# Row minima subtracted by GpSimd and the exponential taken on the way out of PSUM, in a relative-position attention loop

## Chip, cores and metric
The kernel runs as one program on one core of a Trainium2 chip. Its time is that of the device in microseconds (us); lower is better. A core has TensorE (PE, its weight loads are listed as PEld), VectorE (DVE), ScalarE (ACT), GpSimd (POOL) and SyncE (SP), which run their own instruction queues and meet at semaphores, and 16 DMA engines.

## What is computed
The reference is one transformer block over x of 32 batches x 512 tokens x 256 channels: a layer norm, relative-position attention with 16 heads of 16 channels, and an expert layer (8 experts, each takes its 128 best tokens of the 512 of a batch, two products with GELU between, scatter-add). The attention is what matters here:

```python
content_score = jnp.einsum('bhsp,bhtp->bhst', q + u, k)
pos_score = jnp.einsum('bhsp,htp->bhst', q + v, pos)
pos_score = _relative_shift(pos_score)     # pad a column, reshape, drop a row
score = (content_score + pos_score) / jnp.sqrt(jnp.float32(P))
weights = jax.nn.softmax(score, axis=-1)
out = jnp.einsum('bhst,bhtp->bhsp', weights, val)
```

For each of 32 x 16 = 512 (batch, head) pairs the scores are a 512x512 float32 matrix.

## The kernel before
There are two phases, `attention_phase` and `ffn_phase`, with a barrier between them. The attention phase first normalises all batches (to some 185 us) and then runs `ITERS` = 16 unrolled bodies of `BH` = 32 heads (two batches). A head is worked on as TT = 4 tiles of 128 queries x 512 keys. Every engine has its own order, written out by hand in `body(i)`; `kk` is the head within the body and `n = i*BH + kk` its number.

One head passes these stages:

- `position` (PE, L988): four products of the queries with the positions into `xp`, half of the PSUM tensor `quad`, two tiles at a time, LEAD = 5 heads ahead. `x_evacuate` (ACT, L609) copies two tiles at once into a ring in SBUF; SP writes them to DRAM (`write_x`, L411) with rows of 513, and reads them back with rows of 512 (`read_x`, L421) into `shifted`, a ring of NX = 8 heads. This write and read is the relative shift. The read-back of a head follows BEHIND = 2 heads after its write in SP's order.
- `content` (PE, L999): four products of queries and keys into `sp_`, the other half of `quad`, with two banks; tile t waits until the add of tile t-2 is done. `add` (DVE, L761) forms (content + position) x -0.25 in place in `shifted` and the row minimum of it in `mn`.
- `exponential` (ACT, L614): per tile, exp(mn - x) in place in `shifted`.
- `turn` (PE, L1024 and L1025), LAG = 2 heads later: the tiles are transposed by TensorE in two halves of two key blocks; each half fills `tp`, a PSUM tensor of 128x1024 that exists once. `t_evacuate` copies it into `pt` in SBUF: half 0 by DVE (L770, 128x1024), half 1 by DVE (L772, 128x512) and ACT (L623, 128x512) together.
- `times_values` (PE, L1042), three heads behind: products with the values and a column of ones, into `op`; `o_evacuate` (ACT, L630) and `store_o` (SP) once in four heads. The division by the sum happens in the second phase.

Beside this, once in two to sixteen heads, run the projections of the next queries, keys and values (PE L933, L950), their spreading over the partitions (PE L917, L918, evacuated by DVE L734 and L741), and on GpSimd the splits of operands into a high and a low part: `keys` (L504, L506), `queries` (L495, L497) and `split_xt` (L514, L516). After the last body GpSimd issues eight indirect gathers (`gather_tokens`, L92) of the first tokens for the experts.

Of the kernel before, what the change touches and what calls it, by code (L numbers as in the profile page):

```python
# [7 lines left out]
ALU = mybir.AluOpType  # L8
ACT = mybir.ActivationFunctionType
# [11 lines left out]
TT = S // P  # L21
# [118 lines left out]
def attention_phase(nc, x, gate_w, w, w1, w2, consts, xn_d, xt_d, xs_d, att_d, sums_d, shared):  # L140
# [9 lines left out]
    LAG = 2  # L150
# [10 lines left out]
    with ExitStack() as ctx:  # L161
# [65 lines left out]
        def first_keys(n):  # L227

            at = n % 2 * TT
            return pt[:, at:at + 2].rearrange("p c (t r n) -> p (c t) r n", t=TT, r=2)  # L230

        def last_keys(r):
            by_rows = pt[:, 2:4].rearrange("p c (t r n) -> p (c t) r n", t=TT, r=2)
            return by_rows[:, :, r]
# [75 lines left out]
        exp_done = m.sem("exp_done")  # L310
        t_full = m.sem("t_full")
        t_out_dve = m.sem("t_out_dve")
        t_out_act = m.sem("t_out_act")
# [41 lines left out]
        with nc.Block() as block:  # L355
# [121 lines left out]
            def _(pool):  # L477
# [39 lines left out]

                split_xt(0, 0)
# [7 lines left out]
                def body(i):  # L526
                    last = isinstance(i, int) and i == ITERS - 1
                    for kk in range(BH):
                        t = kk // MH + 1
                        if kk % MH == 4 and not (last and t >= TILES):  # L530
                            keys(i, t)
# [17 lines left out]
            def _(act):  # L549
# [61 lines left out]
                def exponential(i, kk, t):  # L611

                    act.wait_ge(added, (i * BH + kk) * TT + t + 1)
                    act.activation(shifted[:, kk % NX, t], shifted[:, kk % NX, t], ACT.Exp, bias=mn[:, kk % NX, t:t + 1],  # L614
                                   scale=-1.0).then_inc(exp_done, 1)

                def t_evacuate(i, kk):

                    n = i * BH + kk
                    act.wait_ge(t_full, (n + 1) * TT)  # L620

                    wait(act, o_full, n)
                    act.activation(last_keys(1), tp[:, 1], ACT.Copy).then_inc(t_out_act, 1)  # L623
# [20 lines left out]
                exponential(0, 0, 0)  # L644

                def body(i):
                    first = isinstance(i, int) and i == 0
                    last = isinstance(i, int) and i == ITERS - 1
                    for kk in range(BH):
# [3 lines left out]
                        if not (first and kk == 0):  # L653
                            exponential(i, kk - 1, 1)
                            exponential(i, kk - 1, 2)
# [6 lines left out]
                        if not (first and kk == 0):  # L662
                            exponential(i, kk - 1, 3)
                            exponential(i, kk, 0)
                        if positions:
                            x_evacuate(i, kk + LEAD, 1)
                        if not (first and kk < LAG):
                            t_evacuate(i, kk - LAG)
# [5 lines left out]
                for t in range(1, TT):  # L674
                    exponential(ITERS, -1, t)
                for k in range(LAG):
                    t_evacuate(ITERS, k - LAG)
# [3 lines left out]
            def _(dve):  # L681
# [83 lines left out]
                def t_evacuate(i, kk, t):  # L765
                    n = i * BH + kk
                    dve.wait_ge(t_full, n * TT + (2, 4)[t])
                    wait(dve, o_full, n - 1 + t)
                    if t == 0:
                        dve.tensor_copy(first_keys(n), tp[:, :, :].rearrange("p r (k n) -> p k r n", k=2 * TT)).then_inc(t_out_dve, 1)  # L770
                    else:
                        dve.tensor_copy(last_keys(0), tp[:, 0]).then_inc(t_out_dve, 1)  # L772

# [74 lines left out]
                def body(i):  # L848
                    first = isinstance(i, int) and i == 0
                    last = isinstance(i, int) and i == ITERS - 1  # L850
                    for kk in range(BH):
                        even, odd = even_group(kk, last), odd_group(kk, last)
                        values = values_at(kk, last)
                        turning = not (first and kk < LAG)
                        add(i, kk, 1)
                        add(i, kk, 2)
                        if turning:
                            t_evacuate(i, kk - LAG, 0)
# [7 lines left out]
                        if turning:  # L866
                            t_evacuate(i, kk - LAG, 1)
# [12 lines left out]
                for k in range(LAG):  # L880
                    for t in range(2):
                        t_evacuate(ITERS, k - LAG, t)

            @block.tensor
            def _(pe):
# [125 lines left out]
                def turn(i, kk, half):  # L1011
                    n = i * BH + kk
                    pe.wait_ge(exp_done, (n + 1) * TT)

                    if half == 0:
# [610 lines left out]
```

## Time and profile before
| | |
|---|---|
| median of 3 runs | 4721.12 us (4718.89 to 4722.01) |
| profiled execution | 4728.36 us |
| its span on the core | 4726.5 us |
| busy in the span | PE 4382.3 us (93%), DVE 3530.2 (75%), ACT 3360.7 (71%), POOL 1261.8 (27%) |
| mean DMA rate | 294 GB/s over the span |

The profile shows one execution. A busy PE is not a PE at its peak, since matmuls are pipelined and their ends are modelled; spans on POOL are rough. The granted clock of TensorE is given as a share of 2.4 GHz, so that a stretch at 1.2 GHz reads 0.50. "Idle before" is the time in which an engine stood still just ahead of a group of instructions, with what ended it. The DMA share is the mean busy share of the 16 DMA engines; it can read a little over 1.

### The profile page before, as it was taken

The page shows a single profiled execution, that of the slowest core. Times are in us where ns is not written, and L with a number is a line of the kernel's source. Part 1 is how long each engine was busy: PE and PEld are TensorE (multiplying, and loading weights), DVE is VectorE, ACT ScalarE, POOL GpSimd, SP SyncE. Part 2 cuts the span into 40 slices and gives each one's busy share as a digit, 9 for nine tenths or more (in the row PEclk, how much of TensorE's full clock was granted, in tenths as well). Part 3 has the DMA queues.
Part 4 walks back from the last instruction along what each step waited for, and adds up shares of the span by engine and source line. Part 5 has one row for each costly group of instructions (what it writes and reads, how often), then busy time and mean ns, then how long its engine had stood idle before and what let it go on. Part 6 is the DMA issues. An engine that isn't in the chain of part 4 may idle for free. (4 is left out here: it accounts for less than half of the span.)

```text
span 4726.5 us, 126083 instructions
## 1 busy us (share of the span) xinstructions
PE 4382.3 (93%) x50100; PEld 3473.8 (73%) x50100; DVE 3530.2 (75%) x7282; ACT 3360.7 (71%) x5120; POOL 1261.8 (27%) x905
## 2 busy tenths in 40 slices
PE   7899999999989989989999999899999999999997
PEld 3466666666666667666667666589999999999997
DVE  7699999998999989999998989744454555434344
ACT  3599999998989999999898999744343433344454
POOL 0111111111111111111111111135565565644443
PEclk9799999999999999999999999999999999999999
DMA  8999999999999999999999999873454545433259
GB/s 330 343 387 387 391 386 385 397 385 383 390 390 388 386 387 390 392 386 385 388 395 382 394 388 385 320 247 77 117 144 110 140 117 128 108 55 86 45 169 311
DMA packets 467858, 1391.46 MB, mean 294 GB/s; under 512 B 59216, under 2 KB 136656, under 8 KB 467024
## 3 DMA queue, kind: packets, MB, share of 16 engines
q1 hardware_dynamic: 418128, 1316.25, 73.9%
q0 software_dynamic: 49152, 67.14, 8.0%
q8 instruction: 407, 6.67, 0.6%
q14 instruction: 171, 1.40, 0.1%
HBM read 708.93 MB, written 674.23 MB: 293 GB/s over the span
## 5 line engine op out<-in xcount | busy, mean ns | idle before, releaser
L761 DVE CUSTOM_DVE_ANT_0 att_shifted<-att_quad,att_shifted 128x512 f32<-128x512 f32 x2048 | 1336.6, 684 | 109.2 <-DMA att_shifted<-xs_d 70.3
L614 ACT ACTIVATE att_shifted<-att_shifted,att_mn 128x512 f32<-128x512 f32 x2048 | 1376.1, 733 | 0.6 <-DVE att_mn L761 0.6
L609 ACT ACTIVATE ring<-att_quad 128x1024 f32<-128x1024 f32 x1024 | 1055.5, 1031 | 261.4 <-PE att_quad L988 240.1
L999 PE MATMUL att_quad<-att_kd,att_qd 64*128 64x512 f32 x2048 | 848.5, 460 | 177.1 <-DVE att_mn L761 171.2
L1483 DVE TENSOR_TENSOR ffn_hp<-ring,ffn_hp 128x512 fp32r<-128x512 f32 x512 | 477.6, 933 | 685.3 <-ACT ring L1420 642.0
L1418 ACT ACTIVATE ffn_hp<-ffn_up 128x512 fp32r<-128x512 f32 x512 | 305.9, 597 | 914.5 <-PE ffn_up L1564 896.8
L988 PE MATMUL att_quad<-att_pos,att_qd 64*128 64x512 f32 x2048 | 862.5, 449 | 15.2 <-ACT ring L609 13.9
L1024 PEld LDWEIGHTS att_tp<-ident,att_shifted 64*128 64x128 f32 x8192 | 647.0, 142 | 272.3 <-ACT att_shifted L614 117.4
L1525 PE MATMUL ffn_yp<-ffn_w2p,ffn_hp 128*128 128x256 f32 x6144 | 827.8, 284 | 3.4 <-DVE ffn_hp L1483 1.7
L1525 PEld LDWEIGHTS ffn_yp<-ffn_w2p,ffn_hp 128*128 128x128 f32 x6144 | 798.7, 191 | 41.0 <-DVE ffn_hp L1483 3.8
L1564 PE MATMUL ffn_up<-ffn_xp,ffn_w1p 128*128 128x512 f32 x3072 | 795.1, 394 | 2.8 <-DVE ffn_xp L1443 2.8
L1024 PE MATMUL att_tp<-ident,att_shifted 64*128 64x64 f32 x8192 | 725.4, 229 | 68.4 <-DVE att_pt L770 23.8
L1025 PE MATMUL att_tp<-ident,att_shifted 64*128 64x64 f32 x8192 | 777.3, 232 | 2.4 <-issue 2.3
L1025 PEld LDWEIGHTS att_tp<-ident,att_shifted 64*128 64x128 f32 x8192 | 653.1, 142 | 18.5 <-issue 6.2
L770 DVE COPY att_pt<-att_tp 128x1024 f32<-128x1024 f32 x512 | 624.5, 1220 | 5.3 <-PE att_tp L1025 2.3
L999 PEld LDWEIGHTS att_quad<-att_kd,att_qd 64*128 64x128 f32 x2048 | 363.0, 190 | 354.1 <-DVE att_mn L761 259.4
L1358 POOL DMA_INDIRECT ffn_d<-ring,picks x256 | 431.8, 1687 | 696.2 <-DVE ring L1451 682.6
L1564 PEld LDWEIGHTS ffn_up<-ffn_xp,ffn_w1p 128*128 128x128 f32 x3072 | 546.4, 190 | 93.6 <-DVE ffn_xp L1443 3.2
L1042 PE MATMUL att_op<-att_pt,att_val 128*17 128x128 f32 x16384 | 601.6, 290 | 4.2 <-issue 3.8
L1042 PEld LDWEIGHTS att_op<-att_pt,att_val 128*17 128x17 f32 x16384 | 427.7, 102 | 60.0 <-issue 8.2
L504 POOL CAST att_kc<-att_qn 128x512 fp32r<-128x512 f32 x64 | 39.4, 616 | 1589.2 <-PE att_mp L918 1580.2
L988 PEld LDWEIGHTS att_quad<-att_pos,att_qd 64*128 64x128 f32 x2048 | 370.6, 190 | 92.2 <-issue 45.4
(125 smaller groups left out, 4992.6 us busy)
## 6 DMA issues: line engine op xcount, KB each, us to landing
xs_d<-ring SPq DMA_DIRECT2D x1024, 513.0 KB, 8.5
att_shifted<-xs_d SPq DMA_DIRECT2D x1024, 512.0 KB, 8.8
att_shifted<-in_L_attn_x_dram SPq DMA_DIRECT2D x32, 512.0 KB, 7.0
xn_d<-att_shifted SPq DMA_DIRECT2D x32, 512.0 KB, 6.4
xt_d<-att_shifted SPq DMA_DIRECT2D x32, 512.0 KB, 7.5
gathered<-xt_d SPq DMA_DIRECT2D x32, 512.0 KB, 9.7
att_d<-att_osb SPq DMA_DIRECT2D x512, 32.0 KB
ring<-in_L_ffn_w_dram SPq DMA_DIRECT2D x16, 1024.0 KB
```

The lines of the kernel that those rows point to most:

```text
L609: act.activation(xo[:, kk % NW, 2 * half:2 * half + 2, 1:S + 1], xp[:, :, :], ACT.Copy).then_inc(x_out, 1)
L614: act.activation(shifted[:, kk % NX, t], shifted[:, kk % NX, t], ACT.Exp, bias=mn[:, kk % NX, t:t + 1], scale=-1.0).then_inc(exp_done, 1)
L761: dve.tensor_tensor_reduce(out=shifted[:, kk % NX, t], in0=sp_[:, t % 2], in1=shifted[:, kk % NX, t], scale=-0.25, scalar=-NEG, op0=ALU.ad ...
L770: dve.tensor_copy(first_keys(n), tp[:, :, :].rearrange("p r (k n) -> p k r n", k=2 * TT)).then_inc(t_out_dve, 1)
L988: ins = pe.matmul(xp[:, t % 2, :], qd[rows, n // GH % ND, t * P:(t + 1) * P], pos[rows, kk // GH % NG8, :], start=True, stop=True)
L999: pe.matmul(sp_[:, t % 2, :], qd[rows, n // GH % ND, t * P:(t + 1) * P], kd[rows, kk // GH % 2, :], start=True, stop=True).then_inc(s_full, 1)
L1024: low = pe.transpose(tp[:, 0, at], shifted[0:ROWS, kk % NX, t, keys], ident[0:ROWS, 0:ROWS])
L1025: high = pe.transpose(tp[:, 1, at], shifted[ROWS:P, kk % NX, t, keys], ident[ROWS:P, ROWS:P])
L1042: ins = pe.matmul(op[32 * t:32 * t + HD + 1, kk % QH * P:(kk % QH + 1) * P], val[:, kk // H % 2, c, kk % H, :], pt[:, of_keys(n, c), t * P ...
L1483: dve.tensor_tensor(hp[:, g % 2, 1, f], hf[:, f % 2], hp[:, g % 2, 0, f].bitcast(F32), ALU.subtract).then_inc(h_low, 1)
L1525: ins = pe.matmul(yp[:, k % 2, 0:D], hp[:, g % 2, hi, f, k * CAP:(k + 1) * CAP], w2p[:, wi, f, :], start=(f == 0 and s == 0), stop=(f == F ...
L1564: ins = pe.matmul(up[:, f % 4, :], w1p[:, wi, c, f * P:(f + 1) * P], xp[:, g % 2, xi, c, :], start=(s == 0 and c == 0), stop=(s == 2 and c ...
```

## The change
The exponential no longer runs in place in SBUF. GpSimd subtracts the row minimum of each tile in place (`subtract_least`, four per head, first in its order for every head). TensorE transposes the differences. ACT then takes exp(-x) while it copies `tp` to `pt`: two instructions of 128x1024 per head, one per half, both from PSUM to SBUF. The four exponentials from SBUF to SBUF, DVE's two copies and ACT's copy are gone. The semaphores `exp_done`, `t_out_dve` and `t_out_act` give way to `lowered` and `t_out`. In `pt` both of a half's key blocks now have the same layout.

```diff
--- before.py
+++ after.py
@@ -224,14 +224,10 @@
         xp, sp_ = quad[:, 0], quad[:, 1]
         tp = m.ps("tp", [P, 2, S])
 
-        def first_keys(n):
-
-            at = n % 2 * TT
+        def turned_keys(n, half):
+
+            at = 2 if half else n % 2 * TT
             return pt[:, at:at + 2].rearrange("p c (t r n) -> p (c t) r n", t=TT, r=2)
-
-        def last_keys(r):
-            by_rows = pt[:, 2:4].rearrange("p c (t r n) -> p (c t) r n", t=TT, r=2)
-            return by_rows[:, :, r]
 
         def of_keys(n, c):
 
@@ -307,10 +303,9 @@
         x_shifted = [m.sem(f"x_shifted{k}") for k in range(NX)]
         s_full = m.sem("s_full")
         added = m.sem("added")
-        exp_done = m.sem("exp_done")
+        lowered = m.sem("lowered")
         t_full = m.sem("t_full")
-        t_out_dve = m.sem("t_out_dve")
-        t_out_act = m.sem("t_out_act")
+        t_out = m.sem("t_out")
         o_full = m.sem("o_full")
         o_out = m.sem("o_out")
         o_stored = [m.sem(f"o_stored{k}") for k in range(2)]
@@ -515,6 +510,12 @@
                     wait_alone(pool, xt_high, b + 1)
                     pool.tensor_tensor(xt[:, s, 1], xf[:, :, :], xt[:, s, 0].bitcast(F32), ALU.subtract).then_inc(xt_low, 1)
 
+                def subtract_least(i, kk, t):
+
+                    pool.wait_ge(added, (i * BH + kk) * TT + t + 1)
+                    pool.tensor_scalar(shifted[:, kk % NX, t], shifted[:, kk % NX, t], mn[:, kk % NX, t:t + 1], None,
+                                       ALU.subtract).then_inc(lowered, 1)
+
                 split_xt(0, 0)
                 queries(0, 0)
                 keys(0, 0)
@@ -527,6 +528,8 @@
                     last = isinstance(i, int) and i == ITERS - 1
                     for kk in range(BH):
                         t = kk // MH + 1
+                        for r in range(TT):
+                            subtract_least(i, kk, r)
                         if kk % MH == 4 and not (last and t >= TILES):
                             keys(i, t)
                         if kk % MH == 6 and t % 2 and not last:
@@ -608,19 +611,14 @@
                     act.wait_ge(x_full, (i * BH + kk) * 2 + half + 1)
                     act.activation(xo[:, kk % NW, 2 * half:2 * half + 2, 1:S + 1], xp[:, :, :], ACT.Copy).then_inc(x_out, 1)
 
-                def exponential(i, kk, t):
-
-                    act.wait_ge(added, (i * BH + kk) * TT + t + 1)
-                    act.activation(shifted[:, kk % NX, t], shifted[:, kk % NX, t], ACT.Exp, bias=mn[:, kk % NX, t:t + 1],
-                                   scale=-1.0).then_inc(exp_done, 1)
-
-                def t_evacuate(i, kk):
+                def exponential(i, kk, half):
 
                     n = i * BH + kk
-                    act.wait_ge(t_full, (n + 1) * TT)
-
-                    wait(act, o_full, n)
-                    act.activation(last_keys(1), tp[:, 1], ACT.Copy).then_inc(t_out_act, 1)
+                    act.wait_ge(t_full, n * TT + 2 * (half + 1))
+
+                    wait(act, o_full, n - 1 + half)
+                    act.activation(turned_keys(n, half), tp[:, :, :].rearrange("p r (k n) -> p k r n", k=2 * TT), ACT.Exp,
+                                   scale=-1.0).then_inc(t_out, 1)
 
                 def o_evacuate(i, q):
                     u = i * QUADS + q
@@ -641,7 +639,6 @@
                 x_evacuate(0, LEAD - 1, 0)
                 x_evacuate(0, LEAD - 1, 1)
                 keep_queries(0, 1)
-                exponential(0, 0, 0)
 
                 def body(i):
                     first = isinstance(i, int) and i == 0
@@ -650,31 +647,27 @@
                         positions = not (last and kk + LEAD >= BH)
                         queries = query_tile(kk - 1, last) if kk else None
                         keys = key_tile(kk - 1, last) if kk else None
-                        if not (first and kk == 0):
-                            exponential(i, kk - 1, 1)
-                            exponential(i, kk - 1, 2)
+                        turning = not (first and kk < LAG)
                         if queries is not None:
                             keep_queries(i, queries)
                         if keys is not None:
                             keep_keys(i, keys)
                         if positions:
                             x_evacuate(i, kk + LEAD, 0)
-                        if not (first and kk == 0):
-                            exponential(i, kk - 1, 3)
-                            exponential(i, kk, 0)
+                        if turning:
+                            exponential(i, kk - LAG, 0)
                         if positions:
                             x_evacuate(i, kk + LEAD, 1)
-                        if not (first and kk < LAG):
-                            t_evacuate(i, kk - LAG)
+                        if turning:
+                            exponential(i, kk - LAG, 1)
                         if kk % QH == 2 and not (first and kk < QH):
                             o_evacuate(i, kk // QH - 1)
 
                 for i in range(ITERS):
                     body(i)
-                for t in range(1, TT):
-                    exponential(ITERS, -1, t)
                 for k in range(LAG):
-                    t_evacuate(ITERS, k - LAG)
+                    for half in range(2):
+                        exponential(ITERS, k - LAG, half)
                 o_evacuate(ITERS - 1, QUADS - 1)
 
             @block.vector
@@ -761,15 +754,6 @@
                     dve.tensor_tensor_reduce(out=shifted[:, kk % NX, t], in0=sp_[:, t % 2], in1=shifted[:, kk % NX, t], scale=-0.25,
                                              scalar=-NEG, op0=ALU.add, op1=ALU.min,
                                              accum_out=mn[:, kk % NX, t:t + 1]).then_inc(added, 1)
-
-                def t_evacuate(i, kk, t):
-                    n = i * BH + kk
-                    dve.wait_ge(t_full, n * TT + (2, 4)[t])
-                    wait(dve, o_full, n - 1 + t)
-                    if t == 0:
-                        dve.tensor_copy(first_keys(n), tp[:, :, :].rearrange("p r (k n) -> p k r n", k=2 * TT)).then_inc(t_out_dve, 1)
-                    else:
-                        dve.tensor_copy(last_keys(0), tp[:, 0]).then_inc(t_out_dve, 1)
 
                 def pick(n):
 
@@ -851,11 +835,8 @@
                     for kk in range(BH):
                         even, odd = even_group(kk, last), odd_group(kk, last)
                         values = values_at(kk, last)
-                        turning = not (first and kk < LAG)
                         add(i, kk, 1)
                         add(i, kk, 2)
-                        if turning:
-                            t_evacuate(i, kk - LAG, 0)
                         if even is not None:
                             kd_evacuate(i, even)
                         if odd is not None:
@@ -863,8 +844,6 @@
                         add(i, kk, 3)
                         if not (last and kk == BH - 1):
                             add(i, kk + 1, 0)
-                        if turning:
-                            t_evacuate(i, kk - LAG, 1)
                         if values:
                             stage_v(i, *values)
                         if lists_at(i, kk):
@@ -877,9 +856,6 @@
 
                 for i in range(ITERS):
                     body(i)
-                for k in range(LAG):
-                    for t in range(2):
-                        t_evacuate(ITERS, k - LAG, t)
 
             @block.tensor
             def _(pe):
@@ -1010,13 +986,9 @@
 
                 def turn(i, kk, half):
                     n = i * BH + kk
-                    pe.wait_ge(exp_done, (n + 1) * TT)
-
-                    if half == 0:
-                        wait(pe, t_out_dve, n * 2)
-                        wait(pe, t_out_act, n)
-                    else:
-                        pe.wait_ge(t_out_dve, n * 2 + 1)
+                    pe.wait_ge(lowered, (n + 1) * TT)
+
+                    wait(pe, t_out, n * 2 + half)
                     for c in range(2):
                         keys = slice((2 * half + c) * P, (2 * half + c + 1) * P)
                         for t in range(TT):
@@ -1034,10 +1006,8 @@
 
                         wait(pe, o_out, i * QUADS + kk // QH)
                     for c in range(TT):
-                        if c < TT - 1:
-                            pe.wait_ge(t_out_dve, n * 2 + (1, 1, 2)[c])
-                        if c >= 2:
-                            pe.wait_ge(t_out_act, n + 1)
+                        if c % 2 == 0:
+                            pe.wait_ge(t_out, n * 2 + c // 2 + 1)
                         for t in range(TT):
                             ins = pe.matmul(op[32 * t:32 * t + HD + 1, kk % QH * P:(kk % QH + 1) * P], val[:, kk // H % 2, c, kk % H, :],
                                             pt[:, of_keys(n, c), t * P:(t + 1) * P], start=(c == 0), stop=(c == TT - 1))
```

## Rows read from the trace of the kernel before

**Rows 1.** The page: busy time of engines; DMA rate in 40 slices of the span
```profile
PE 4382.3 (93%) x50100; PEld 3473.8 (73%) x50100; DVE 3530.2 (75%) x7282; ACT 3360.7 (71%) x5120; POOL 1261.8 (27%) x905
...
GB/s 330 343 387 387 391 386 385 397 385 383 390 390 388 386 387 390 392 386 385 388 395 382 394 388 385 320 247 77 117 144 110 140 117 128 108 55 86 45 169 311
```

**Rows 2.** Windows: length; busy us (instructions) PE, PEld, DVE, ACT, POOL; PEclk; DMA share; GB/s
```profile
300.00:3000.00 2700.00, 2467.53 (x37038) 1828.77 (x37036) 2465.18 (x5510) 2466.24 (x3609) 379.24 (x303) 0.96 1.01 388
1640.00:1720.00 80.00, 72.75 (x1117) 53.47 (x1117) 75.09 (x170) 75.59 (x111) 12.58 (x10) 1.00 1.02 401
```

**Rows 3.** Windows of 20 us, the same columns
```profile
1280.00:1300.00 20.00, 19.48 (x294) 14.47 (x292) 19.23 (x44) 19.91 (x31) 4.34 (x4) 1.00 1.03 408
...
1740.00:1760.00 20.00, 16.79 (x231) 11.69 (x230) 15.75 (x38) 16.43 (x26) 5.92 (x5) 0.83 1.03 402
1760.00:1780.00 20.00, 18.44 (x286) 13.89 (x286) 18.10 (x40) 16.98 (x25) 0.23 (x1) 0.91 0.93 343
```

**Rows 4.** Waits, 300 to 3000 us: total us, times, longest
```profile
ACT ring L609 <- PE att_quad L988: 215.2, 259, 2.5
PE att_quad L999 <- DVE att_mn L761: 159.7, 359, 2.1
...
DVE att_shifted L761 <- DMA att_shifted<-xs_d: 68.3, 122, 2.0
...
PE att_tp L1024 <- DVE att_pt L770: 21.7, 53, 0.4
```

**Rows 5.** Groups by line and shape, 300 to 3000 us
```profile
L614 ACT ACTIVATE att_shifted<-att_shifted,att_mn 128x512 f32<-128x512 f32 x1926 | 1294.9, 733 | 0.0
L761 DVE CUSTOM_DVE_ANT_0 att_shifted<-att_quad,att_shifted 128x512 f32<-128x512 f32 x1924 | 1255.7, 684 | 98.3 <-DMA att_shifted<-xs_d 68.3 <-PE att_quad L999 25.7
L609 ACT ACTIVATE ring<-att_quad 128x1024 f32<-128x1024 f32 x962 | 991.8, 1031 | 227.4 <-PE att_quad L988 215.2
...
L770 DVE COPY att_pt<-att_tp 128x1024 f32<-128x1024 f32 x482 | 587.9, 1220 | 2.5 <-remote 1.4
...
L772 DVE COPY att_pt<-att_tp 128x512 f32<-128x512 f32 x481 | 329.8, 686 | 0.2 <-PE att_tp L1024 0.2
L623 ACT ACTIVATE att_pt<-att_tp 128x512 f32<-128x512 f32 x481 | 289.3, 601 | 5.5 <-PE att_tp L1025 1.6
```

**Rows 6.** DMA issues of the page: KB each, median us from issue to landing
```profile
att_shifted<-xs_d SPq DMA_DIRECT2D x1024, 512.0 KB, 8.8
```

**Rows 7.** POOL's groups over the span, and L504's durations (min/median/max)
```profile
L497 POOL TENSOR_TENSOR att_qc<-att_qn,att_qc 128x512 fp32r<-128x512 f32 x64 | 99.3, 1552 | 5.1
L506 POOL TENSOR_TENSOR att_kc<-att_qn,att_kc 128x512 fp32r<-128x512 f32 x64 | 81.8, 1278 | 5.1
...
L516 POOL TENSOR_TENSOR att_xt<-gathered,att_xt 128x1024 fp32r<-128x1024 f32 x32 | 77.1, 2410 | 2.6
L495 POOL CAST att_qc<-att_qn 128x512 fp32r<-128x512 f32 x64 | 72.6, 1134 | 786.1 <-PE att_mp L918 677.6 <-ACT att_qn L573 108.5
...
L514 POOL CAST att_xt<-gathered 128x1024 fp32r<-128x1024 f32 x32 | 33.4, 1044 | 201.4 <-DMA gathered<-xt_d 201.4
...
L504 POOL CAST att_kc<-att_qn x60: 609/612/619, 300.6 to 2950.0; 128x512 fp32r<-128x512 f32 x60
```

**Rows 8.** Timeline: first and last of the eight gathers, and what stood still
```profile
2996.82 1.17 POOL L92 DMA_INDIRECT gathered<-xn_d,picks  x1 [0.16 <-issue]
...
3005.82 0.95 POOL L92 DMA_INDIRECT gathered<-xn_d,picks  x1 [0.30 <-issue]
...
3008.47 0.75 DVE L734 TENSOR_SCALAR att_qd<-att_mp,att_marks 128x512 fp32r<-128x512 f32 x1 [7.50 <-remote]
3008.58 1.02 ACT L609 ACTIVATE ring<-att_quad 128x1024 f32<-128x1024 f32 x1 [8.43 <-remote]
```

**Rows 9.** Timeline: the last add, and the first instruction of the expert phase
```profile
3061.37 0.69 DVE L761 CUSTOM_DVE_ANT_0 att_shifted<-att_quad,att_shifted 128x512 f32<-128x512 f32 x1
...
3077.44 2.57 ACT L1388 ACTIVATE ffn_w1p<-ring 128x256 fp32r<-128x256 f32 x8 [5.73 <-PEq L355]
```

## Prediction, made before the changed kernel was run
> **What bounds the kernel now.** I read the page first: its busy shares [rows 1] are means over two phases that have nothing in common. PE, DVE and ACT look alike at 71 to 93% and POOL idle at 27%; the reader should take from them only that the last 16 of the 40 slices (the experts) hold little of DVE and ACT, and that the slices before them carry a flat 385 to 395 GB/s. The change touches only the attention loop, 512 heads in some 2,870 us, so I cut that out with the windows view [rows 2]. Over 2,700 us it ran 481 heads (962 evacuations by L609, two a head [rows 5]), a period of 2700/481 = 5.613 us. In a period PE is busy 2467.5/481 = 5.13 us, DVE 5.13, ACT 5.13, POOL 379.2/481 = 0.79; the DMA share is 1.01 and the rate 388 GB/s, so a head moves 388 x 5.613 = 2.18 MB. Three engines at 91% and the DMA engines at 101%: four candidates.
>
> Short windows tell them apart [rows 3]. The rate is not flat. Its best 20 us has 408 GB/s at share 1.02 to 1.03, an undisturbed 80 us holds 401 [rows 2], and 1740 to 1780 shows what happens between: first the DMA is full (1.03, 402 GB/s) while DVE does only 15.8 of 20 us and PE's granted clock falls to 0.83, then the share falls to 0.93 and the rate to 343. The two sides take turns: engines wait for a transfer, PE loses its clock, the engines catch up with three of them near 95% busy, and meanwhile feed the queue too slowly. The waits [rows 4] say the same: DVE waits for the read-back 68.3 us (122 times), ACT for PE 215.2 us, PE for DVE's adds 159.7 us. So the DMA rate is the floor, a full queue at about 401 GB/s, and the engines' lack of slack costs the difference to 388. A read-back lands 8.8 us after its issue [rows 6] and is worth 0.52 MB/388 GB/s = 1.35 us: some six transfers are under way at a time, a deep queue.
>
> **The change part by part, per head, at the spacings of busy stretches.**
> DVE loses L770 (1.22 us) and L772 (0.69) [rows 5]; as back-to-back instructions overlap by some 0.07, that is 1.77 of 5.13: about 3.4 us remain.
> ACT loses four exponentials of 0.733 and L623 of 0.601 [rows 5], 3.53 us of durations. It gains two exponentials of 128x1024 from PSUM. The nearest row is L609, the same shape, source and engine, Copy instead of Exp: 1.031 us. From above I bound it by twice L614, 1.47 us. I take 1.03, since function aside the instruction is L609's (and the per-partition bias that L614 carries is gone): 2.06 us added, ACT at 5.13 - 3.53 + 2.06 = 3.7 us, at the upper bound 4.5. Either way under 5.4: hidden.
> PE issues the same transposes and products. Its waits change owner: turn() waits for `lowered` and `t_out`. Half 1 of a head now needs ACT's exponential of half 0, which stands behind one evacuation: 2 x 1.03 = 2.1 us after the last position matmul, and PE has about 3 us of other work there. The first turn of the next head needs the exponential of half 1, again 2.1 us, against about 1.8 us of work: I add 0.2 us. PE's need is then 5.13 + 0.2 = 5.3 us, with the 159.7/481 = 0.33 us of waits for adds and the 0.05 for L770 [rows 4] mostly gone, since DVE no longer has copies between adds. At nothing saved PE stays where it is.
> POOL gains four in-place subtractions of 128x512 with a per-partition scalar, 2,048 in all, each behind `added`. No row shows a POOL tensor_scalar. From below the cast of that shape, one input: 0.612 us [rows 7]. From above the two-input subtraction of that shape: 1.278 (1.552 with a permuted operand, which this one has not) [rows 7]. With 0.08 us between instructions, four cost 2.8 to 5.4 us, POOL in all 3.6 to 6.2. I take the lower end, since the operation has one tensor input as the cast has, and allow up to 0.8 us each: POOL 4.3 us of 5.4. The two ends fall on opposite sides of the DMA's floor, and the price at which POOL becomes the bound is (5.46 - 0.79)/4 = 1.17 us.
> The Trainium skill speaks against the move: its "GPSIMD Engine Reference", section "Engine selection", keeps elementwise arithmetic on VectorE, GpSimd being about twice as slow with two inputs, though roughly at line rate with one. By its one-input figure of 1.03 cycles an element at 1.2 GHz (section on side-by-side cycle accounting) the estimate would be 0.44 us plus the dispatch, by its two-input figure of 2.6 cycles 1.1 us plus it. The trace agrees in both columns (0.612 and 1.278 us); whether a scalar from memory counts as an input neither says.
>
> **What stands behind the waiting POOL.** Its queue also holds keys(), queries() and split_xt(); they now wait for the subtractions in front. The longest run is split_xt (1.04 + 2.41) then the next head's four and queries (1.13 + 1.55): at 0.7 us each POOL is some 1 us late in that stretch, at 1.0 us some 3.4. A head's subtractions are due about 1.7 periods (9 us) after its last add, queries and keys a full head after they are ready, split_xt a batch ahead. So the lateness is covered; without this cover each us late would land once in 16 heads, 32 us in all. SP's reads wait for `t_full` of a head four turns back, so neither SP queue order nor transfers move.
> At the phase's end POOL's eight indirect gathers for the experts are moved past the last 20-odd heads' subtractions. Before, they ran from 2996.8 to 3006.8 in the midst of full DMA, and DVE and ACT stood still for 7.5 and 8.4 us beside them [rows 8]; nothing else in the loop shows that. They would now follow the last subtraction, some 0.7 us after the last add, and take 8 x 1.25 = 10 us plus landing; between the last add and the first expert instruction lie 3077.4 - 3062.0 = 15.4 us [rows 9]. They just fit, while no large transfer runs. I count 5 us gained (0 to 8); 3 us lost if landing sticks out.
> The tail itself (turn, then a copy or now an exponential, one after the other) is equal within 2 us.
>
> **Sum.** With slack on DVE, ACT and PE (3.4, 3.7, 5.3 us) the DMA is the sole floor: 2.18 MB at 401 GB/s is 5.43 us; PE's clock dips will still cost something, so I take 399, 5.46 us. Saved: (5.613 - 5.46) x 505 heads in the steady part = 77 us, rounded with the 5 at the end to 80. Span 4726.5 - 80 = 4646.5. The profiled execution took 4728.36 us, 7 over the median of the runs; I subtract from the median: 4721 - 80 = 4641.
> Bounds of the DMA floor: at 408 GB/s (its best 20 us) 5.34 us, -138 and with the end -145: 4576; at 388 nothing.
>
> **Rivals.**
> (a) The DMA is already full (share 1.01) and the rate is what this mixture gives; engines faster or not, the alternation stays because DMA waits still drop PE's clock. For it: the mean share is within 2% of the best seen. Against it: the dips to 343 GB/s at share 0.93, which follow stretches short of engine time. Time 4721 - 0 to 9. Chance 0.15.
> (b) POOL becomes the bound: a subtraction costs the two-input price. 4 x 1.36 + 0.79 = 6.23 us a head, (6.23 - 5.613) x 505 = +312: 5033. It decides from (5.613 - 0.79)/4 = 1.21 us each on. For it: in place and with a second operand from SBUF; against: the cast. Chance 0.14.
> (c) DVE and POOL exclude each other in SBUF. Adds and subtractions in turn would give 2.7 + 2.8 + 0.8 = 6.3 us and the same 5,060 or so. Against it: POOL's cast took 609 to 619 ns in all 60 cases [rows 7] beside a DVE that was 91% busy. The Trainium skill, "SBUF — State Buffer", gives an exclusive lock of a shared port pair when DVE has two SBUF inputs or a 2-port mode; L761 has one input in PSUM, and by that rule nothing is blocked. Chance 0.04.
> (d) PE becomes the bound through the single `tp` (exponentials later than I count): PE at 5.5 us instead of 5.3, -57 and the 5: about 4660 to 4700. Chance 0.17, counted as faster.
> My forecast has 0.50: DMA the floor, 4590 to 4660.
>
> **How the numbers follow.** About 0.2% (9 us) is what a measurement of this kernel can tell. Faster 0.67 (forecast and d); same 0.14; slower 0.19 (b, c and a little of a). The range 4585 to 4735 takes in forecast, (d) and (a), and leaves out (b), (c) and the far end of 408 GB/s: 0.2. The forecast's own range is 4590 to 4660.
>
> **What would show it.** The page of after: POOL tensor_scalar 128x512 at 0.6 to 0.8 us, POOL at 3.6 to 4.3 us a head; ACT's exponential 128x1024 near 1.03; DVE and ACT 60 to 70% busy in 300 to 2900; the DMA share at 1.02 to 1.03 and 397 to 403 GB/s, with DVE's waits for the read-back longer than 68 us, and PE's waits for adds due to the DMA alone; no stop near the gathers. Wrong if POOL is over 90% busy (b, c), if GB/s stay at 388 with the same dips (a), or if PE waits mainly for the exponential (d).

## The result and the profile after

The changed kernel takes 5407.06 us (median; 5405.49 to 5408.54) against 4721.57 us of the kernel before on the same chip: ratio 1.1449, 95% interval 1.1435 to 1.1464. It is 686 us slower where 80 us faster were forecast. The profiled execution has a span of 5406.8 us.

From the page of the changed kernel: the rows that answer to [rows 1], GpSimd's subtraction, ACT's new exponential, and the large transfers, of which [rows 6] shows the second:

```profile
PE 4592.9 (85%) x50100; PEld 3610.5 (67%) x50100; DVE 2665.9 (49%) x6258; ACT 2892.2 (53%) x3584; POOL 4409.2 (82%) x2953
...
GB/s 342 310 318 310 312 315 309 313 317 314 308 319 309 312 317 309 316 311 317 313 302 319 314 313 311 313 317 273 151 112 116 136 134 118 134 81 54 71 127 305
...
L516 POOL TENSOR_SCALAR att_shifted<-att_shifted,att_mn 128x512 f32<-128x512 f32 x2048 | 3162.4, 1575 | 0.0
...
L620 ACT ACTIVATE att_pt<-att_tp 128x1024 f32<-128x1024 f32 x1024 | 1046.6, 1022 | 486.7 <-PE att_tp L997 283.4
...
xs_d<-ring SPq DMA_DIRECT2D x1024, 513.0 KB, 6.4
att_shifted<-xs_d SPq DMA_DIRECT2D x1024, 512.0 KB, 6.9
```

Its windows and waits, 300 to 3600 us (columns as in [rows 2] and [rows 4]):

```profile
300.00:3600.00 3300.00, 2629.10 (x36499) 1930.65 (x36498) 1631.42 (x4486) 1995.90 (x2133) 3287.28 (x2193) 0.86 0.88 313
```
```profile
DVE att_qd L727 <- PE att_mp L894: 1011.6, 237, 8.2
ACT ring L612 <- PE att_quad L964: 832.2, 610, 3.5
...
PE att_tp L996 <- POOL att_shifted L516: 495.3, 276, 4.8
...
DVE att_shifted L754 <- DMA att_shifted<-xs_d: 0.8, 2, 0.4
```

Read POOL first. It is busy 3287 of 3300 us, and stands idle 0.0 us before its subtractions. In 3300 us it does 1897 of them, 474 heads, so a head takes 6.96 us (5.613 before). A subtraction lasts 1.575 us; from start to start they are 1.542 apart (the last 29 in one run take 44.73 us). 4 x 1.542 + 0.79 us of POOL's old work = 6.96 us: the period is POOL's and nothing else's. (6.96 - 5.613) x 505 heads = 680 us, nearly the whole loss of 686. Some 5 us more lie behind the loop: from the start of the last add to DVE's first instruction of the expert phase pass 21.8 us, where 16.5 passed before, since POOL is still subtracting 8 us after the last add. Everyone else waits in a chain: PE for POOL, ACT and DVE for PE, and the read-back, 68.3 us of DVE's waits in [rows 4], is now always in time (0.8 us). The rate falls from 388 to 313 GB/s and the granted clock from 0.96 to 0.86, as consequences.

### The profile page after: what moved, and what is told of

It is laid out like the page before. It is cut to its first block and busy times, and to the rows that moved or that the text cites. A ratio compares the mean times of both kernels' runs of the same rounds, so it can differ in the third digit from the quotient of the medians.

```text
span 5406.8 us, 124548 instructions
## 1 busy us (share of the span) xinstructions
PE 4592.9 (85%) x50100; PEld 3610.5 (67%) x50100; DVE 2665.9 (49%) x6258; ACT 2892.2 (53%) x3584; POOL 4409.2 (82%) x2953
## 5 line engine op out<-in xcount | busy, mean ns | idle before, releaser
L516 POOL TENSOR_SCALAR att_shifted<-att_shifted,att_mn 128x512 f32<-128x512 f32 x2048 | 3162.4, 1575 | 0.0
L996 PE MATMUL att_tp<-ident,att_shifted 64*128 64x64 f32 x8192 | 853.1, 246 | 545.1 <-POOL att_shifted L516 533.3
L620 ACT ACTIVATE att_pt<-att_tp 128x1024 f32<-128x1024 f32 x1024 | 1046.6, 1022 | 486.7 <-PE att_tp L997 283.4
L996 PEld LDWEIGHTS att_tp<-ident,att_shifted 64*128 64x128 f32 x8192 | 729.2, 154 | 744.2 <-POOL att_shifted L516 684.3
L975 PE MATMUL att_quad<-att_kd,att_qd 64*128 64x512 f32 x2048 | 904.8, 484 | 124.6 <-DVE att_mn L754 120.7
L964 PE MATMUL att_quad<-att_pos,att_qd 64*128 64x512 f32 x2048 | 891.0, 467 | 19.2 <-ACT ring L612 17.7
L997 PE MATMUL att_tp<-ident,att_shifted 64*128 64x64 f32 x8192 | 851.5, 246 | 0.0
L997 PEld LDWEIGHTS att_tp<-ident,att_shifted 64*128 64x128 f32 x8192 | 727.1, 154 | 45.0 <-issue 11.5
L727 DVE TENSOR_SCALAR att_qd<-att_mp,att_marks 128x512 fp32r<-128x512 f32 x256 | 192.2, 751 | 1091.8 <-PE att_mp L894 1091.8
L1012 PE MATMUL att_op<-att_pt,att_val 128*17 128x128 f32 x16384 | 695.7, 323 | 0.3 <-ACT att_pt L620 0.2
L975 PEld LDWEIGHTS att_quad<-att_kd,att_qd 64*128 64x128 f32 x2048 | 404.5, 205 | 292.2 <-DVE att_mn L754 186.5
L1012 PEld LDWEIGHTS att_op<-att_pt,att_val 128*17 128x17 f32 x16384 | 473.8, 112 | 85.4 <-ACT att_pt L620 0.6
```

Of the source, the lines that this page charges most:

```text
L516: pool.tensor_scalar(shifted[:, kk % NX, t], shifted[:, kk % NX, t], mn[:, kk % NX, t:t + 1], None, ALU.subtract).then_inc(lowered, 1)
L620: act.activation(turned_keys(n, half), tp[:, :, :].rearrange("p r (k n) -> p k r n", k=2 * TT), ACT.Exp, scale=-1.0).then_inc(t_out, 1)
L964: ins = pe.matmul(xp[:, t % 2, :], qd[rows, n // GH % ND, t * P:(t + 1) * P], pos[rows, kk // GH % NG8, :], start=True, stop=True)
L975: pe.matmul(sp_[:, t % 2, :], qd[rows, n // GH % ND, t * P:(t + 1) * P], kd[rows, kk // GH % 2, :], start=True, stop=True).then_inc(s_full, 1)
L996: low = pe.transpose(tp[:, 0, at], shifted[0:ROWS, kk % NX, t, keys], ident[0:ROWS, 0:ROWS])
L997: high = pe.transpose(tp[:, 1, at], shifted[ROWS:P, kk % NX, t, keys], ident[ROWS:P, ROWS:P])
```

## The experiments

**Theory A**: the loss is POOL's price alone. **Rival B**: the longer chain through the single `tp` costs as well. A second question goes with it, since a cheap subtraction had been forecast to gain 80 us: what would the kernel be worth with POOL out of the way?

### e1: no subtraction

```diff
-                        for r in range(TT):
-                            subtract_least(i, kk, r)
...
-                    pe.wait_ge(lowered, (n + 1) * TT)
+                    pe.wait_ge(added, (n + 1) * TT)
```

> The changed kernel without the subtraction on GpSimd; the turn waits for the adds instead, and the exponential is taken of the values as they are (the row minimum is left out). Theory A, that the 6.96 us a head of the changed kernel are POOL's own 4 x 1.542 + 0.79: the period falls to the floor of the DMA engines that I forecast, 5.40 to 5.50 us, and the time to 4610 to 4665 us, the DMA rate to 397 to 403 GB/s. Rival B, that the longer chain through the single tp (transpose, exponential, next transpose) holds PE back: the period stays over 5.7 us, over 4770 us, with PE waiting for the exponential. Rival C, that the DMA engines gave all they had in the kernel before: 5.61 us, 4710 to 4730 us.

Measured: 4708.3 us, ratio to before 0.9958 (0.9941 to 0.9974). Windows and waits of this run, 300 to 3000 us:

```profile
300.00:3000.00 2700.00, 2426.28 (x37188) 1823.00 (x37184) 1684.58 (x4567) 2013.31 (x2174) 384.05 (x308) 0.96 1.01 391
```
```profile
ACT ring L610 <- PE att_quad L962: 644.9, 770, 2.5
...
PE att_quad L973 <- DVE att_mn L752: 243.8, 455, 5.5
DVE att_shifted L752 <- DMA att_shifted<-xs_d: 192.7, 289, 2.3
```

Without POOL's subtraction the loss is gone, so A holds for the loss and B falls: PE waits 9.6 us in all for an exponential before a transpose. But A's 4610 to 4665 us were missed, and so were its 397 to 403 GB/s. The time is 2 us below the range of rival C (4710 to 4730): the gain, 20 us by the ratio, is a quarter of the forecast. DVE and ACT have fallen from 91% to 62 and 75% busy, and the DMA engines do 391 GB/s in place of 388 at the same share of 1.01. The slack has gone into waiting: DVE waits for the read-back 192.7 us, where it was 68.3 [rows 4], and PE for the adds behind it 243.8 us, where it was 159.7. That is the mechanism of rival (a) of the prediction.

### e2: a copy in POOL's place

```diff
-                    pool.tensor_scalar(shifted[:, kk % NX, t], shifted[:, kk % NX, t], mn[:, kk % NX, t:t + 1], None,
-                                       ALU.subtract).then_inc(lowered, 1)
+                    pool.tensor_copy(shifted[:, kk % NX, t], shifted[:, kk % NX, t]).then_inc(lowered, 1)
```

> The changed kernel with a copy in place of each subtraction on GpSimd (the row minimum is left out); waits and order are kept. Theory A: POOL needs 4 x 0.62 + 0.79 = 3.3 us a head and is hidden; the time is that of the kernel without any subtraction within 15 us. Rival B', that the wait behind POOL (its place in the chain, the queue with the splits) costs something of its own whatever the instruction's price: more than 30 us above the kernel without subtraction.

4717.31 us, ratio 0.9971 (0.9962 to 0.9981), 9 us above e1, whose interval it overlaps. The copy takes 615 ns. In the two traces the last add starts at the same time (3042.2 and 3042.4 us); the 9 us lie behind the loop (see e9). So POOL's place in the chain costs nothing in the loop that can be told; the price does.

### e3, e11, e4: what makes the subtraction dear

```diff
-                    pool.tensor_scalar(..., mn[:, kk % NX, t:t + 1], None, ALU.subtract)
+ e3                pool.tensor_scalar(..., 0.5, None, ALU.subtract)
+ e11               pool.tensor_scalar(..., 1.0, None, ALU.mult)
+ e4                pool.tensor_tensor(..., mn[:, kk % NX, t:t + 1].to_broadcast([P, S]), ALU.subtract)
```

> The changed kernel with the constant 0.5 subtracted in place of the row minimum (which is left out). If the 1.575 us come from the scalar operand in memory: 0.6 to 0.9 us each and the time of the copy. If they come from the operation itself on GpSimd: 1.5 to 1.6 us each and 5380 to 5410 us.

> The changed kernel with a multiplication by the constant 1 in place of the subtraction (the row minimum is left out), to see whether GpSimd's price for tensor_scalar hangs on the operation. If it is the instruction's own: 1.49 us each as with the constant subtracted, 5220 to 5250 us. If subtraction is the dear case: under 1 us and 4710 us.

> The changed kernel with the subtraction written as tensor_tensor with the minimum broadcast along the row. If the two-input form costs what L501 and L506 show: 1.28 us each, 1.25 from start to start, a period of 4 x 1.25 + 0.79 = 5.79 us and 4721 + 0.18 x 505 = 4810 us (4780 to 4850), faster than the changed kernel by 600 us, slower than the one before. If a broadcast operand is as dear as the scalar: 1.55 us and 5400 us.

Measured: e3 5235.87 us (ratio 1.1074, 1.1055 to 1.1092), e11 5236.09 us (one run), e4 4716.0 us (0.9974, 0.9964 to 0.9983). The groups of POOL, one row each from e3 (300 to 3000 us), e11 (whole span) and e4 (300 to 3000 us):

```profile
L516 POOL TENSOR_SCALAR att_shifted<-att_shifted 128x512 f32<-128x512 f32 x1631 | 2381.3, 1493 | 0.0
```
```profile
L516 POOL TENSOR_SCALAR att_shifted<-att_shifted 128x512 f32<-128x512 f32 x2048 | 2986.5, 1492 | 0.0
```
```profile
L516 POOL TENSOR_TENSOR att_shifted<-att_shifted,att_mn 128x512 f32<-128x512 f32 x1938 | 1961.5, 1043 | 366.7 <-DVE att_mn L754 364.4
```

e3 fitted neither of my cases (0.6 to 0.9 us, or 1.5 to 1.6 us and 5380 to 5410 us). Between them: the scalar from memory makes 0.08 us, the operation nothing; the instruction form itself is dear on GpSimd, 1.49 us where a copy of the shape takes 0.615. The same subtraction written with two tensors, the second a broadcast, takes 1.043 us. That missed my expectation of 1.25 on the good side: a broadcast operand is cheaper than a full one (1.278 in [rows 7]; that instruction also writes fp32r, but so does the cast of 0.612 us, and a copy without it takes 0.615). POOL then needs 4 x 1.04 + 0.79 = 5.0 us, less than the period, and idles 366.7 us waiting for the adds. This one line makes the changed kernel some 690 us faster, and a little faster than the one before. In the traces, from the start of the first add to that of the last, the loop takes 2875.4 us before, 2852.1 in e1 and 2847.6 in e4: 23 and 28 us less. Behind the loop e4 gives 11 us back (see e9).

### e10: the subtraction on DVE

```diff
+                def lower(i, kk, t):
+                    wait_alone(dve, added, n * TT + t + 1)
+                    dve.tensor_scalar(shifted[:, kk % NX, t], shifted[:, kk % NX, t], mn[:, kk % NX, t:t + 1], None,
+                                      ALU.subtract).then_inc(lowered, 1)
...
                         add(i, kk, 1)
+                        lower(i, kk - 1, 3)
+                        lower(i, kk, 0)
                         add(i, kk, 2)
+                        lower(i, kk, 1)
```

(GpSimd's loop is taken out as in e1; tile 2 is lowered behind the add of tile 3, and tile 3 behind the add of tile 1 of the next head.)

> The changed kernel with the subtraction on DVE, in place from SBUF to SBUF, behind its adds (GpSimd is out of it). DVE, at 3.5 us a head without it, gains four instructions of 0.35 to 0.7 us: 4.9 to 6.3 us. Theory D: if they cost under 0.5 us each, DMA stays the floor and the time is that without subtraction, 4700 to 4725. At 0.68 each, the price of its other 128x512 instructions, DVE is at 6.2 us and the time at 4950 to 5050.

4805.95 us, ratio 1.017 (1.0155 to 1.0186): between the two cases.

```profile
L760 DVE TENSOR_SCALAR att_shifted<-att_shifted,att_mn 128x512 f32<-128x512 f32 x1861 | 986.6, 551 | 0.0
```

551 ns each brings DVE to 2432.9/465.75 heads = 5.2 us of a period of 5.80 us. The read-back is no longer waited for (0.4 us in all) and the rate is 376 GB/s, so the DMA engines do not set this period. DVE and PE, each 90% busy, wait for one another: PE 245.6 us for DVE's adds, DVE 265 us for PE. The place on DVE is 90 us worse than the two-tensor form on POOL.

### e5, e6: fewer bytes

Theory D, from e1: the DMA engines were the floor of the kernel before. To move that floor alone, one tile in four is not read back (the add takes what its slot holds).

```diff
-                    rows = slice(2 * half, 2 * half + 2)
+                    rows = slice(2 * half, 2 * half + (2 if i * BH + kk < NX else 2 - half))
```

> The kernel before with one tile in four not read back from DRAM (from the ninth head on; the add takes what the slot holds), 12% fewer bytes: 1.92 MB a head, at 391 GB/s 4.91 us. Nothing is changed on the engines, which need 5.13 us each on PE, DVE and ACT. If the DMA engines are the floor of the kernel before (rival a of the prediction, now theory D): the period falls to the engines' 5.2 to 5.4 us, 4720 - 110 to 4720 - 210, 4510 to 4610 us. If the engines and their waits set it: 4700 to 4725 us.

> The same 12% fewer bytes read back, in the changed kernel with the two-tensor subtraction. Theory D: the floor is now PE, 5.0 to 5.2 us a head, 4450 to 4520 us, below the light kernel before by 40 us or more, since DVE and ACT have slack here: what the change would bring where the DMA engines leave room. If the chain through POOL and the single tp holds: no faster than the light kernel before.

e5 4607.01 us (0.975, 0.9732 to 0.9768), e6 4537.18 us (0.9601, 0.9581 to 0.9621). Windows of e5 and of e6, 300 to 2900 us:

```profile
300.00:2900.00 2600.00, 2419.00 (x37186) 1817.58 (x37186) 2464.26 (x5532) 2463.83 (x3624) 382.77 (x306) 0.99 0.98 356
```
```profile
300.00:2900.00 2600.00, 2397.61 (x37995) 1810.40 (x37994) 1697.18 (x4652) 2048.50 (x2231) 2359.15 (x2283) 0.99 0.99 364
```

With nothing changed on any engine the kernel before gains 118 us by the ratio, and e5 lies just within theory D's 4510 to 4610: its floor was the DMA engines. In e5 DVE and ACT are 95% busy and the read-back is waited for 9.9 us: now mainly the engines hold, though the DMA share is still 0.98. In e6 they are relieved, and that is worth 70 us there, where it is worth 12 to 20 with all bytes (e4, e1, by their ratios). e6 missed its range by 17 us; the half-size transfers cost the DMA engines more per byte than I reckoned (share 0.99 at 364 GB/s, where 388 GB/s took 1.01), so it is near its floor again.

### e7, e12: less of PE

The forecast's floor was 401 GB/s; e1 has 391. Either PE's lateness holds it down (D1) or the mixture of transfers does (D2). In e7 two key blocks of four are left out of the products with the values; in e12 three of four transposes as well. Both stand on e4, and neither computes the whole attention.

```diff
                     for c in range(TT):
                         ...
+                        if c in (1, 2):
+                            continue
...
+ e12                   for t in range(TT) if n < 2 else (TT - 1,):
```

> The changed kernel with the two-tensor subtraction, with two of four key blocks left out of the products with the values: 0.5 us less of PE a head, the bytes unchanged. Theory D1, that the alternation between a full queue and a late PE keeps the rate at 391 GB/s: with PE at 4.6 us the rate rises to 398 GB/s or more and the time falls by 35 to 80 us under the 4716 of the same kernel with all products. Theory D2, that 391 GB/s is what the DMA engines do with this mixture of transfers: within 12 us of 4716.

> The kernel of the run with two of four key blocks left out of the products with the values, and now from the third head on three of four transposes left out as well (tp keeps old values): PE at about 3.7 us a head, so that no engine is near the period; the bytes are unchanged. What is left is the DMA engines' own rate for this mixture. Theory D2 (its ceiling is under the 401 GB/s that I forecast): 393 to 397 GB/s, 5.49 to 5.54 us, 4655 to 4685 us, close to the 4680 of the run with less PE. Theory D1 (PE's lateness holds the rate down): 400 GB/s or more, under 4645 us.

e7 4679.84 us (0.9903, 0.9888 to 0.9918), e12 4667.54 us (0.9865, 0.9844 to 0.9885). Windows of e7 and e12, 300 to 2900 us:

```profile
300.00:2900.00 2600.00, 2301.74 (x28600) 1640.92 (x28596) 1637.13 (x4435) 1954.49 (x2110) 2254.10 (x2169) 0.92 1.02 393
```
```profile
300.00:2900.00 2600.00, 2345.56 (x17461) 1510.12 (x17453) 1646.11 (x4460) 1963.70 (x2124) 2260.12 (x2181) 0.76 1.02 394
```

Much less work on PE lifts the rate from 390 to 393 and 394, at a share of 1.02. e7 fitted neither theory: 36 us under e4 is D1's time (35 to 80) and three times what D2 allowed (12), but 393 GB/s is short of D1's 398. The traces take the 36 us apart: the loop, from first to last add, is 16 us shorter than e4's (2831.5 against 2847.6), 10 us come from behind it, where e4 has a stop and e7 has none (see e9), and 8 from a first add that came earlier. e12 lies in D2's ranges (393 to 397 GB/s, 4655 to 4685 us), with a loop of 2814.0 us. It is not the clean case that I wanted: with half of e4's matmuls gone (17461 in the window, 35890 in e4's) PE's granted clock fell to 0.76, so that PE stayed 90% busy and DVE's adds waited for it 205.1 us. So D2 is favoured, and D1 not excluded: that 401 GB/s, held for 80 us in one stretch [rows 2], can be held throughout has been seen in no run.

### e8: the small stores from ACT's queue

The eight small stores of four heads (`store_o`) leave SP's queue and are issued by ACT, two a head, on top of e4.

```diff
-                        if kk % QH == 0 and not (first and kk < 2 * QH):
-                            store_o(i, kk // QH - 2)
...
+                        u, part = divmod(i * BH + kk - QH - 3, QH)
+                        if u >= 0:
+                            store_part(u // QUADS, u % QUADS, part)     # act.dma_start of att_d and sums_d, tile part
```

> The changed kernel with the two-tensor subtraction and the eight small stores of four heads issued from ACT's queue, two a head, in place of eight in a row in SP's queue (4.3 us in which SP issues no other transfer). If the dips in the DMA rate come from SP standing in these stores: 15 to 50 us faster than 4716. If SP's queue is not what limits: within 10 us of 4716, or slower by ACT's 1 us a head if ACT were short, which it is not.

4704.76 us, ratio 0.9955 (0.9941 to 0.9968). The median is 11 us under e4's, at the edge of both expectations, and the two intervals against before overlap, so the stores' own share is not shown. The rate is 390 GB/s as in e4, and the traced loop is no shorter (2850.2 us against 2847.6); what the trace gains it gains behind the loop. It is the fastest kernel here that computes everything, 21 us under the one before in its own rounds.

### e9: the gathers behind the loop, in the kernel before

```diff
                 pool.wait_ge(xt_low, B)
+                pool.wait_ge(added, B * H * TT)
```

> The kernel before, with GpSimd waiting for the last add before it issues the eight gathers (they then run behind the attention loop, as in the changed kernel). If the 7.5 us in which DVE and ACT stand still near 3000 us come from the gathers in the midst of full DMA, as the prediction has it: that stop is gone and the time falls by 3 to 9 us, 4712 to 4720. If it is no effect of the gathers: the stop stays at the same place and the time within 2 us.

4725.74 us, ratio 1.0001 (0.9992 to 1.001): no gain beyond 4 us, though the stop is gone. The gathers begin behind the last add, and ACT waits no longer than 3.6 us in what is left of the loop after 2950 us; in e1, where they come early again, ACT has its stop of 8.3 us (rows of e9's timeline and of e1's groups, 2990 to 3010 us):

```profile
3061.88 1.17 POOL L92 DMA_INDIRECT gathered<-xn_d,picks  x1 [59.22 <-DVE att_mn L762]
```
```profile
L610 ACT ACTIVATE ring<-att_quad 128x1024 f32<-128x1024 f32 x8 | 8.2, 1028 | 12.2 <-remote 8.3 <-PE att_quad L962 3.9
```

So the stop goes with the gathers, and its worth in the loop was read wrongly. While the engines stood, the DMA engines worked on (first row below, from the kernel before: DVE and ACT idle, share 1.03), and the expert phase begins within 1 us of e9's (3077.9 and 3077.1 us).

That it comes from gathers in the midst of full DMA, as the prediction has it, is not borne out. e5 and e10 issue them in the loop, e5 at a share of 1.03 (second row), and nothing stands still. e2 and e4 issue them behind the loop, and ACT stands still for 8.35 and 10.05 us, at a share of some 0.4 (last rows, from e4). What the engines wait for stays open.

```profile
3004.00:3008.00 4.00, 1.20 (x10) 1.04 (x10) 0.00 (x0) 0.00 (x0) 2.16 (x3) 0.60 1.03 412
```
```profile
2888.00:2892.00 4.00, 3.22 (x62) 2.28 (x58) 3.82 (x9) 3.92 (x7) 2.99 (x4) 1.00 1.03 370
```
```profile
3046.00:3050.00 4.00, 0.00 (x0) 0.00 (x0) 0.00 (x0) 0.00 (x0) 3.09 (x4) 0.63 0.39 108
```
```profile
3052.02 1.02 ACT L620 ACTIVATE att_pt<-att_tp 128x1024 f32<-128x1024 f32 x1 [10.05 <-remote]
```

Behind the loop the stop is not taken back. From the start of the last add to DVE's first instruction of the expert phase pass 16.5 us before, 16.7 in e1 and 17.6 in e7, but 25.4 in e2 and 27.7 in e4. That is the 9 us of e2 over e1, and it takes two fifths of what e4's loop gains.

## Why the prediction was wrong

**The step that failed** is POOL's price. "I take the lower end, since the operation has one tensor input as the cast has, and allow up to 0.8 us each" against 1.575 us. The number of inputs did not order the prices: cast 0.61, broadcast pair 1.04, full pair 1.28, tensor_scalar 1.49 to 1.58 us, all of one shape. It also lies outside the bound that I called "from above". That bound was the dearest unpermuted POOL instruction of the shape that the trace had, and nothing made it a bound. By this term alone the period is 6.96 us instead of 5.46. (The 0.08 us that I put between instructions did not appear either: 1.575 us each, 1.542 from start to start.)

**The rival (b)** named the mechanism, the place and the point from which it decides (1.21 us each; measured 1.575). Its sum with the true price gives 4 x 1.54 + 0.79 and the measured 5407 within 6 us. I gave it 0.14 and, by the false bound, 5033 us, so even the rival's own time was 374 us short. (c), mutual exclusion of DVE and POOL, did not occur: the 2,048 subtractions took 1552 to 1617 ns, the last 29, partly beside a resting DVE, 1579 to 1598, and DVE's adds 0.685 us as before.

**The gain with POOL out of the way** was mis-sized too: 5.43 us a head at 401 GB/s; e1 gives 391 GB/s, 20 us by the ratio instead of 80. From one good stretch of 80 us I took a ceiling for 2,870 us. The mean share of 1.01 beside 1.03 in the best 20 us was the better witness: the kernel before was within 2% of full, and e5 shows that this was its floor. Rival (a), at 0.15, is the nearest to what would have happened, though its 0 to 9 us are less than e1 gained. The dips in the rate, which I laid to engines short of slack, stay with DVE 62% busy: e1 still has 20 us windows from 341 to 409 GB/s.

**Right**, by their steps: DVE keeps 1631.4/474 = 3.4 us; ACT's exponential from PSUM takes 1.022 us (1.03 taken). ACT as a whole has 4.2 us, not 3.7; most likely since I took off full durations of instructions that had overlapped. It stayed hidden. PE's wait for the exponential of the other half, counted at 0.2 us a head, is 9.6 us in all in e1, 0.02 a head. keys(), queries() and split_xt() behind the subtractions cost nothing that can be told in e2.

**Wrong, but small**: the gathers behind the loop. Their 5 us of gain are none (e9); in the changed kernel they follow a POOL that is 8 us late, and the expert phase begins 5 us later after the last add than before. In e2 and e4 a stop beside them costs 9 and 11 us. And the expert phase takes the last 14 of the page's 40 slices, not 16; nothing hangs on that.

What stays open: whether the rate of 391 to 394 GB/s is set by the kinds of transfers, and which, or still by PE; and what the engines wait for in the stop beside the gathers.

## What to carry to other kernels

A price from another instruction form is no bound, on GpSimd least of all: before work moves there, that form should be timed alone, and where it lands near the threshold the other spelling of the same arithmetic (here two tensors with a broadcast) tried. When a shared resource reads a share near 1 throughout a loop, relieving engines that are 91% busy buys waits; first ask what the loop does with less of that resource, as e5 did. A stop of the engines that the DMA engines work through, as in the loop of the kernel before, need not be lost time; the same stop where nothing else runs is (e2, e4). And before a difference of 10 us is given to a loop, the loop should be measured alone.

## What the runs showed of the hardware

GpSimd on 128x512 float32 from SBUF to SBUF: copy 0.615 us, tensor_tensor with a broadcast second operand 1.043, with a full one (and fp32r written) 1.278, tensor_scalar with a constant 1.49 whatever the operation (subtract, multiply), with a scalar from memory 1.575. The Trainium skill, "GPSIMD Engine Reference", section "Engine selection", calls one-input work roughly line rate; the copy agrees, tensor_scalar at two and a half times the copy does not. DVE does the same subtraction in 0.551 us. TensorE with less to do was granted less clock, 0.92 and then 0.76 where e4 has 0.96, and stayed 89 and 90% busy at nearly the same period (e7, e12). Eight indirect gathers stopped ACT for 8.4 us in the kernel before and for 10.05 us behind the loop of e4, and not at all in e5, e7 and e10.
